# Two buffers for the rotated rows and inverse norms, the clamp on GpSimd, one layer norm and the output merge placed elsewhere

## The reference, cut to what matters

```
x = x + attn(layernorm(x))        # 16 heads of 8, rotary, causal over 512 tokens
x = x + ffn(layernorm(x))         # two layers of the following
  h = shift_token(x)              # upper half of the features from the token before
  q, k, v = split(h @ wqkv)       # 8 heads of 64
  q = l2norm(q) * qs              # q / max(|q|, 1e-12), the same for k
  q, k = rotary_xpos(q, k)
  o = local_attention(q, k, v)    # blocks of 64 tokens, each sees itself and the block before
  x = x + o @ wo
  h = layernorm(shift_token(x)) * lg + lb
  a, g = split(h @ w1 + b1);  x = x + (a * gelu(g)) @ w2 + b2
```

## Time and profile before

| | |
|---|---|
| median of 3 runs | 2443.62 us (2433.88 to 2451.03) |
| the profiled execution | 2439.99 us, span 2438.2 us, mean granted clock 0.98 |
| PE busy | 2153.6 us (88%) |
| DVE busy | 1763.4 us (72%) |
| POOL busy | 1773.9 us (73%) |
| ACT busy | 1553.0 us (64%) |
| chain that ended last | PE 38%, DVE 21%, ACT 14%, POOL 13%, issue 11% |

### The profile page before, as it was taken

One profiled execution on the slowest core, in us unless ns is written; L12 is line 12 of the kernel. 1 busy time (PEld: TensorE's weight loads), 2 busy tenths in 40 slices (PEclk: granted clock), 3 DMA queues, 4 the chain that ended last, 5 costly groups with the idle time before them and its releaser, 6 DMA issues.

```text
span 2438.2 us, 55022 instructions
## 1 busy us (share of the span) xinstructions
PE 2153.6 (88%) x20736; PEld 1447.8 (59%) x20736; DVE 1763.4 (72%) x4632; ACT 1553.0 (64%) x2510; POOL 1773.9 (73%) x1615
## 2 busy tenths in 40 slices
PE   4887899899999989998999999999899999988886
PEld 1444566665666666665666656666566666665654
DVE  4766777787777877788777777778777777666653
ACT  1445666676676667666766766766676667765553
POOL 2126768787777868787686777878787778788882
PEclk9999999999999999999999999999999999999997
DMA  4222121121212111121112112121121211111110
GB/s 138 65 66 54 40 53 49 44 59 45 57 37 60 52 46 49 48 59 46 49 49 59 44 45 58 33 64 51 39 51 47 60 48 36 25 32 27 28 25 23
DMA packets 115081, 119.56 MB, mean 49 GB/s; under 512 B 31945, under 2 KB 88054, under 8 KB 114818
## 3 DMA queue, kind: packets, MB, share of 16 engines
q1 hardware_dynamic: 114818, 116.04, 18.2%
HBM read 55.96 MB, written 20.97 MB: 32 GB/s over the span
## 4 chain that ended last, share of the span: by engine, by line
PE 38%; DVE 21%; ACT 14%; POOL 13%; issue 11%; DMA 1%; SPq 1%; ACTq 0%; DVEq 0%; POOLq 0%
PE ps L734 4%; PE ps L645 4%; POOL inv L1408 4%; DVE ps L977 4%; PE ps L554 4%; PE ps L828 3%; DVE nm L1019 3%; PE ps L587 3%; DVE ss L1029 3%; PE ps L712 3%; PE ps L600 2%; PE ps L567 2%; ACT PT L1190 2%; PE ps L810 2%; PE ps L819 2%
## 5 line engine op out<-in xcount | busy, mean ns | idle before, releaser
L977 DVE CUSTOM_DVE_ANT_0 ps<-ps,causal 128x512 f32<-128x512 f32 (+3 forms) x1024 | 492.4, 506 | 328.3 <-PE ps L587 322.3
L1408 POOL TENSOR_TENSOR inv<-ss,nhalf 128x16 f32<-128x16 f32 x128 | 377.7, 2950 | 394.0 <-DVE QN L1012 394.0
L1190 ACT ACTIVATE PT<-ps 128x512 f32<-128x512 f32 (+1 forms) x768 | 409.1, 536 | 352.5 <-PE ps L602 349.8
L587 PE MATMUL ps<-KA,QA 72*128 72x512 bf16 (+3 forms) x1024 | 275.1, 311 | 77.1 <-DVE nmax L977 72.9
L1397 POOL TENSOR_TENSOR RS<-RAW,rot 128x512 f32<-128x512 f32 x256 | 319.9, 1271 | 0.0
L1403 POOL TENSOR_TENSOR RC<-RC,RS 128x1024 f32<-128x1024 f32 x128 | 300.9, 2351 | 18.4
L600 PE MATMUL ps<-QA,KA 75*128 75x512 bf16 (+3 forms) x1024 | 286.8, 306 | 27.8 <-ACT PT L1190 26.0
L1386 POOL TENSOR_TENSOR RC<-RAW,rot 128x1024 f32<-128x1024 f32 x128 | 307.9, 2405 | 0.0
L1019 DVE TENSOR_REDUCE nm<-ps 128x8 f32<-128x1024 f32 x128 | 156.4, 1222 | 119.3 <-PE ps L734 119.3
L699 PE MATMUL ps<-wqkv,ZT 128*128 128x512 f32 x512 | 241.9, 595 | 0.0
L587 PEld LDWEIGHTS ps<-KA,QA 72*128 72x128 bf16 x1024 | 96.4, 100 | 235.3 <-DVE nmax L977 142.4
(11 more groups left out here) (122 smaller groups left out, 5304.9 us busy)
## 6 DMA issues: line engine op xcount, KB each, us to landing
V_even<-V_odd SPq DMA_DIRECT2D x256, 130.0 KB, 2.6
QA<-parts SPq DMA_DIRECT2D x192, 96.0 KB
KA<-parts SPq DMA_DIRECT2D x192, 96.0 KB
parts<-qkp SPq DMA_DIRECT2D x32, 384.0 KB, 3.5
X_next<-in_x SPq DMA_DIRECT2D x16, 256.0 KB, 3.1
X<-in_x SPq DMA_DIRECT2D x16, 256.0 KB, 2.9
x_kept<-X SPq DMA_DIRECT2D x16, 256.0 KB, 3.8
XR<-x_kept SPq DMA_DIRECT2D x32, 128.0 KB, 2.9
```

The lines of the kernel that those rows point to most:

```text
L587: last = pe.matmul(dst[:, c0:c0 + w], QA[e][0:QK_ROWS, h % UNIT, qt * P:(qt + 1) * P], KA[e][0:QK_ROWS, h % UNIT, 0:w], start=True, stop=True)
L977: ins = v.tensor_tensor_reduce(for_max(i, x)[:, c0:c0 + w], for_max(i, x)[:, c0:c0 + w], causal[:, S - w:S], -1.0, -NEG, ALU.add, ALU.min, ...
L1190: a.activation(PT1[:, h % UNIT, c0:c0 + w], for_exp(i, x)[:, 0:w], ACT.Exp, scale=SCALE1).then_inc(exped.sem, 1)
L1408: g.tensor_tensor(inv[:, :], ss[:, :], nhalf[:, :], ALU.pow).then_inc(inv_ready.sem, 1)
```

## The change

- `RC` and `inv` get two buffers each, by tile parity. Pool's `rotate_by_cos(m)` and `over_norms(m)` wait for `qn_ready` of tile m-2 instead of m-1.
- The clamp goes from DVE's `norms` to Pool's `over_norms`, ahead of the power. It waits there for `ss_sum`. ACT's `squares` waits for the sum (`ss_sum`) of the tile before instead of for its clamp.
- `first_normalise(.., 0)` moves from the end of Pool's slot 7 to the end of its slot 8, and SP's `load_first(1, 1)`, which waits for it, from slot 8 to slot 10.
- PE's `merge` and DVE's `add_heads` go ahead of attention position 1 instead of behind it.

```diff
-        RC = sb("RC", [P, 2 * INNER])[:, :]
+        RC = [sb(f"RC{n}", [P, 2 * INNER])[:, :] for n in range(2)]
-        inv = sb("inv", [P, 2 * H2])
+        inv = [sb(f"inv{n}", [P, 2 * H2]) for n in range(2)]
...
-                    if s == 8 and lives(i, 1):
+                    if s == 10 and lives(i, 1):
                         sp.wait_ge(*past(ln_out.sem[0], ln_out.at(later(i, 1), 1)))
                         load_first(1, 1)
...
                         project_qk(s + 3)
-                    attention_step(s, 1)
                     if tile_in(i, s - 1):
                         merge(s - 1)
+                    attention_step(s, 1)
                     attention_step(s, 2)
...
                     v.tensor_reduce(ss[:, :], SQ.rearrange("p (h e) -> p h e", e=E2), AX.X,
                                     ALU.add).then_inc(ss_sum.sem, 1)
-                    v.wait_ge(*past(ss_sum.sem, ss_sum.at(i, m + 1)))
-                    v.tensor_scalar(ss[:, :], ss[:, :], 1e-24, None, ALU.max).then_inc(ss_ready.sem, 1)
...
-                    attention_step(s, 1)
                     if tile_in(i, s - 1):
                         add_heads(s - 1)
+                    attention_step(s, 1)
...
-                    a.wait_ge(*past(ss_ready.sem, ss_ready.at(i, m)))
+                    a.wait_ge(*past(ss_sum.sem, ss_sum.at(i, m)))
...
-                    g.wait_ge(*past(qn_ready.sem, qn_ready.at(i, m)))
-                    g.tensor_tensor(RC.rearrange(heads, w=2, h=H2), RAW[m % 2].rearrange(heads, w=2, h=H2),
+                    g.wait_ge(*past(qn_ready.sem, qn_ready.at(i, m - 1)))
+                    g.tensor_tensor(RC[m % 2].rearrange(heads, w=2, h=H2), RAW[m % 2].rearrange(heads, w=2, h=H2),
...
                 def over_norms(m):
+                    g.wait_ge(*past(ss_sum.sem, ss_sum.at(i, m + 1)))
+                    g.tensor_scalar(ss[:, :], ss[:, :], 1e-24, None, ALU.max).then_inc(ss_ready.sem, 1)
                     g.wait_ge(*past(ss_ready.sem, ss_ready.at(i, m + 1)))
-                    g.wait_ge(*past(qn_ready.sem, qn_ready.at(i, m)))
-                    g.tensor_tensor(inv[:, :], ss[:, :], nhalf[:, :], ALU.pow).then_inc(inv_ready.sem, 1)
+                    g.wait_ge(*past(qn_ready.sem, qn_ready.at(i, m - 1)))
+                    g.tensor_tensor(inv[m % 2][:, :], ss[:, :], nhalf[:, :], ALU.pow).then_inc(inv_ready.sem, 1)
...
-                    if s == 7 and lives(i, 1):
+                    if s == 8 and lives(i, 1):
                         first_normalise(later(i, 1), 0)
```

More of the change, by code:

```diff
@@ L1011, in unit_heads @@
                     v.wait_ge(*past(k_tr.sem, k_tr.at(i, m)))
-                    v.tensor_tensor(QN.rearrange("p (h e) -> p h e", e=E2), RC.rearrange("p (h e) -> p h e", e=E2),
-                                    inv[:, :].unsqueeze(2).to_broadcast([P, 2 * H2, E2]),
+                    v.tensor_tensor(QN.rearrange("p (h e) -> p h e", e=E2), RC[m % 2].rearrange("p (h e) -> p h e", e=E2),
+                                    inv[m % 2][:, :].unsqueeze(2).to_broadcast([P, 2 * H2, E2]),
                                     ALU.mult).then_inc(qn_ready.sem, 1)
@@ L1402, in rotate_by_sin @@
                     g.wait_ge(*past(rs_ready.sem, rs_ready.at(i, m + 1)))
-                    g.tensor_tensor(RC, RC, RS, ALU.add).then_inc(added.sem, 1)
+                    g.tensor_tensor(RC[m % 2], RC[m % 2], RS, ALU.add).then_inc(added.sem, 1)
                 def over_norms(m):
+                    g.wait_ge(*past(ss_sum.sem, ss_sum.at(i, m + 1)))
+                    g.tensor_scalar(ss[:, :], ss[:, :], 1e-24, None, ALU.max).then_inc(ss_ready.sem, 1)
                     g.wait_ge(*past(ss_ready.sem, ss_ready.at(i, m + 1)))
-                    g.wait_ge(*past(qn_ready.sem, qn_ready.at(i, m)))
-                    g.tensor_tensor(inv[:, :], ss[:, :], nhalf[:, :], ALU.pow).then_inc(inv_ready.sem, 1)
+                    g.wait_ge(*past(qn_ready.sem, qn_ready.at(i, m - 1)))
+                    g.tensor_tensor(inv[m % 2][:, :], ss[:, :], nhalf[:, :], ALU.pow).then_inc(inv_ready.sem, 1)
                 def tile_normalise(m):
```

## The result

The kernel after takes 2500.11 us, the median of four runs (2491.34 to 2501.57), against 2447.32 for the kernel before in the same series (four runs, 2433.88 to 2452.0). The ratio is 1.022, with a 95% interval from 1.017 to 1.027: slower by some 53 us, where I had forecast no change (2444.0) and a range that ended at 2492. The profiled execution took 2498.95 us, at a mean granted clock of 0.955 where the one before had 0.980.

The account below looks back on a forecast made before the run. A loop within the slot through four engines, none full, was taken as the bound. Ordinary slots at +2.9 us a pair times 6.65 gave +19, the tail -15: 2439.99 + 19 - 15 = 2444.0 us, range 2388 to 2492.

Parts of the forecast that it names:

- In all 2.2 us, on the loop: In slots 4, 6, 12 and 14, Pool's RC delays QN by 1.6 us and L957 by 0.6: cost 8.8 a pair.
- the first rival: QN keeps ahead of RC, so the 8.8 us a pair go: -59 us, 2386; chance 0.22.
- Clamp: Leaving DVE, it gains 4.5 us a pair in even slots and 1.1 in slot 1: 5.6 (4 to 14.9).
- Layer norm: Parts in slot 8 no longer stand behind it: gain 2.0 us a pair (0 to 4); slot 9 loses 0.3.
- QN beside the power isn't held up: In slots 0, 2 and 10 QN falls beside Pool's power, taken not to hold it up.
- What the move frees: L949 in slots 4 and 12 and L1089 in slot 0 no longer meet Pool's addition: gain 3.8 us a pair.
- Odd slots and QN: In odd slots QN meets the second half of RS for about 0.6 us, within the room there.
- Merge: Ahead of position 1 it costs 0.4 us in odd and 0.25 in even slots: 5.2 a pair (-5 to 15).
- Tail: In the last 20 slots, freed power and moved clamp gain 1.5 us per two slots: -15 us (0 to -40).
- QN slips by: QN starts just ahead of RC and is not held: the 8.8 us a pair go, -59 us, 2386; chance 0.22.
- The merge helps: With QN late, PE is idle, so the early merge costs nothing: 35 us fewer, 2410; chance 0.17.
- QN is passed over, slower: Pool's next instruction passes QN; slots 3, 5, 7, 11 and 13 wait for the addition: +67 us, 2511; chance 0.13.

## Why the prediction was wrong

*The step that failed* is "In all 2.2 us, on the loop" with its product "Cost 4 x 2.2 = 8.8" a pair, 59 us in all. The mechanism, the four slots and the phase were right. The term was mis-sized, and twice.

First, the length of the hold-up is not what it costs. I put the 2.2 us on the loop one for one. The trace shows 2.57 us in slot 14, and then PE at half its clock for another 1.9 us, since the hold-up stretches PE's wait from 0.56 to 4.07 us. Filling that wait took 43 us out of the ordinary slots with the hold-up in place; delaying DVE without contention cost 88 us for 59; and removing two holds of 1.84 us gave 41 us for 24. Whatever made the idle time, it was paid for one and a half to one and three quarter times in these three. Nothing in the prediction spoke of the clock: it was 1.00 over the pairs of before, and I took it for granted in slots to which I added a wait. A sign of it stood in the trace of before: in the slot 15 of 20.8 us PE waits 2.52 us, and over the next 4 us the clock is 0.58.

Second, slot 7 was missing from the list. QN takes 3.13 us there. DVE and Pool at its start in after:

```profile
1246.46 3.13 DVE L1012 TENSOR_TENSOR QN<-RC,inv 128x1024 f32<-128x1024 f32 x1
```

```profile
1243.49 2.50 POOL L1395 TENSOR_TENSOR RS<-RAW,rot 128x512 f32<-128x512 f32 x2
1246.13 2.37 POOL L1401 TENSOR_TENSOR RC<-RC,RS 128x1024 f32<-128x1024 f32 x1
```

I had seen QN meeting the second half of RS here. What sets the phase is the end of slot 6. There a small DVE instruction with one input (L931, 0.17 us in before) starts while Pool rotates the next tile, and it ends 0.02 us behind Pool:

```profile
1242.64 0.91 DVE L931 TENSOR_SCALAR first_veps<-first_mv 128x4 f32<-128x4 f32 x1
```

```profile
1241.16 2.37 POOL L1384 TENSOR_TENSOR RC<-RAW,rot 128x1024 f32<-128x1024 f32 x1
```

Slot 7 begins there, so QN, 3.0 us later, comes 0.33 us into the addition each time and is held for nearly the whole of it. It is so in all five pairs of after, and also in the kernel whose PE wait is filled (QN 3.11, slot 7 at 18.5), so PE's slowness isn't the reason. Slot 7 is longer by 2.3 us a pair, 15 us in all. The 0.7 to 1.2 us that L931 loses in slot 6 stood in no term either. The phases had been worked out from the slots of before, in which Pool rotated nothing at that point.

With forecast +19, clock 43 and slot 7 15 the sum is 77, against +75.6 measured. That they meet this closely is partly luck, since smaller errors cancel in it. One slip in the prediction's own figures: its range ends at 2388, though it is said to reach down to the first rival, which stands at 2386. The other steps, one by one:

- *Clamp*: right in slot 1 (-1.5 against -1.1), and in slot 8, where clamp and layer norm together gave 2.4 (2.65 forecast). In slot 14 its 1.22 us are there too, hidden under the rest.
- *Layer norm*: right in sign and size; PE's wait for the parts fell from 17.7 us to 6.0. Slot 9 lost 0.4 (0.3 forecast), but only because inv has two buffers.
- *QN beside the power isn't held up*: not tested as I meant it. In slots 0 and 2 QN starts 0.3 and 0.2 us ahead of the power in three of the five pairs, takes 1.22 to 1.24, and it is the power that grows, to 3.72 and 3.80 us. In the other two pairs, and in slot 10, QN is over before the power starts. In slot 8 QN is 0.2 us ahead of RC and isn't held, as forecast.
- *What the move frees*: right for L949 (749 ns, 0.7 forecast). Wrong for L1087 (L1089 in before) in slot 0: it still takes 1.77 us there in three of the five pairs, where it took 1.94, and slot 0 gained 0.3 instead of 1.1. Its mean over all slots fell from 1074 to 800 ns.
- *Odd slots and QN*: 1.65 in slot 5 and 1.86 in slot 13, the "0.6 us, within the room there"; their lengths grew by 0.3 and 0.5, which the merge explains.
- *Merge*: 27 us alone and 28 in after, against 35; but 0 beside the clamp and layer norm with single buffers. Its odd-slot part was right (0.2 to 0.7 us in slots 3, 5, 7, 11 and 13 of every comparison). Alone, PE's clock in slot 4 and the held clamp in slot 15 add to it.
- *Tail*: right, -17 against -15. The squares are the bound close behind, and just where it was guessed, at half of the 2.97 us. DVE in slot 10 of the last pair of after, against the earlier trace rows:

```profile
2384.17 1.22 DVE L1029 TENSOR_REDUCE ss<-SQ 128x16 f32<-128x1024 f32 x1 [1.52 <-ACT SQ L1219]
```

The rivals: *QN slips by* fell; the kernel with one RC, in which QN takes 1.22 everywhere but L957 is held up in two slots, comes nearest to it (2417.7; 2386 forecast). *The merge helps* fell: it costs in after. *QN is passed over, slower* comes near in time (2511), but not by its mechanism: of its five odd slots only slot 7 waited for an addition, and there because of phase; slots 3 and 11 have QN at 1.22. It comes near for the wrong reason.

What stays open: the odd slots' price of the merge is much the same everywhere (but for slots 1, 9 and 15), but what the other slots add or give back differs with the surroundings. I have read it in the traces of slots 4 and 15 and haven't separated it by a run. Nor did a run show why the clock falls behind one wait and not behind another of the same length.

## What to carry to other kernels

A second buffer for an off-path helper isn't free even when nobody waits for the helper: the wait that it removes may be what kept the helper's SBUF reads away from the path's instructions. Before adding it, lay the helper's new start times over the two-input instructions of the critical engine. Give a second buffer only to what gains from it (here inv), keep the wait where it orders the two engines (here RC), and put the critical engine's two-input instructions back to back so that the helper is the one that waits (here that paid in slots 4 and 12, where the helper reads next, and paid nothing in the kernel before). Lay them over the small one-input instructions at a slot's end too: one of these set the phase of slot 7. Where a delay leaves TensorE idle for microseconds, read the granted clock behind it; where it has fallen, the delay cost about one and a half times its length here.
